# Softmax attention: the products for the maxima on two row groups of TensorE, from a second copy of the stacked queries and keys

## The reference

```
q = (x @ Wq).reshape(b, s, 2, 4, 16)      # s = 1024 tokens of an image
kk = (x @ Wk).reshape(b, s, 2, 16)
v = (x @ Wv).reshape(b, s, 2, 16)
scores = einsum('bqkgd,btkd->bkgqt', q, kk) / 4
attn = softmax(scores, axis=-1)
out = einsum('bkgqt,btkd->bqkgd', attn, v) @ Wo
```

## Time and profile before

| | |
|---|---|
| median of 3 runs | 4212.15 us (4211.81 to 4214.71) |
| profiled execution | 4220.6 us, its span 4218.9 us |
| TensorE matmuls | 3328.1 us busy, 79% |
| TensorE weight loads | 1655.9 us, 39% |
| VectorE | 2950.6 us, 70% |
| ScalarE | 2077.9 us, 49% |
| POOL | 1704.8 us, 40% |

### The profile page before, as it was taken

The page is one execution under the profiler, slowest core; times in us unless marked ns, Lnnn a source line. Parts: engine busy times, 40 slices in busy tenths (PEclk is TensorE's granted clock), DMA queues, the critical chain, the costliest instruction groups (busy, mean ns, idle before and its releaser), DMA issues. The chain is left out here.

```text
span 4218.9 us, 69037 instructions
## 1 busy us (share of the span) xinstructions
PE 3328.1 (79%) x20395; PEld 1655.9 (39%) x20397; DVE 2950.6 (70%) x6280; ACT 2077.9 (49%) x3690; POOL 1704.8 (40%) x2093
## 2 busy tenths in 40 slices
PE   2479999999999999999955999077877778638883
PEld 0212333333332333333224887045555555425552
DVE  7568887878788887888814666557766677546664
ACT  3326666666666666666644776011212212237772
POOL 2111232333232322333234554245666666437772
PEclk9769999999999999999987999589999999869995
DMA  2021111121101111121003332001111111033336
GB/s 94 18 33 25 27 39 37 39 41 40 37 25 26 39 38 38 40 40 39 12 14 112 104 104 95 12 24 37 39 39 38 36 38 38 25 104 102 103 99 255
DMA packets 122360, 226.28 MB, mean 54 GB/s; under 512 B 36048, under 2 KB 41416, under 8 KB 121880
## 3 DMA queue, kind: packets, MB, share of 16 engines
q1 hardware_dynamic: 82776, 142.33, 13.5%
q0 software_dynamic: 33664, 69.27, 5.2%
q10 hardware_dynamic: 5536, 9.99, 0.6%
HBM read 116.99 MB, written 104.50 MB: 52 GB/s over the span
## 5 line engine op out<-in xcount | busy, mean ns | idle before, releaser
L1217 ACT ACTIVATE b_probs<-b_ps_s 128x512 f32<-128x512 f32 x2048 | 1174.0, 596 | 678.0 <-PE b_ps_s L1261 639.4
L1019 DVE TENSOR_REDUCE b_maxes<-b_ps_m 128x1 f32<-128x1024 f32 x1024 | 1216.7, 1215 | 325.1 <-PE b_ps_m L1249 317.8
L1261 PE MATMUL b_ps_s<-b_qs,b_ks 99*128 99x512 bf16 x2048 | 789.8, 389 | 86.7 <-DMA b_qs<-b_m_parts 41.9
L1249 PE MATMUL b_ps_m<-b_ks,b_qs 96*128 96x512 bf16 x2048 | 639.8, 395 | 68.6 <-DVE b_maxes L1019 47.3
L1273 PE MATMUL b_ps_o<-b_probs,b_vs 128*32 128x512 f32 x4096 | 549.4, 609 | 23.3 <-ACT b_probs L1217 22.8
L1261 PEld LDWEIGHTS b_ps_s<-b_qs,b_ks 99*128 99x128 bf16 x2048 | 198.8, 98 | 884.5 <-ACT b_probs L1217 685.2
L938 POOL DMA_INDIRECT slots_in<-b_xn,b_slot x256 | 250.9, 980 | 416.4 <-ACT b_probs L1217 369.8
L1893 POOL DMA_INDIRECT pair_rows<-e_y_out,e_xin x284 | 284.5, 1002 | 131.9 <-issue 83.5
L2531 POOL DMA_INDIRECT cards_in<-d_cards,d_slot x256 | 251.7, 983 | 179.7 <-DVE d_slot L2809 93.0
L2463 POOL DMA_INDIRECT d_y<-slots_out,d_slot_now x256 | 246.3, 962 | 142.1 <-DVE d_inner L2694 65.2
L1249 PEld LDWEIGHTS b_ps_m<-b_ks,b_qs 96*128 96x128 bf16 x2048 | 191.8, 100 | 242.5 <-DVE b_maxes L1019 113.4
(11 more groups left out here) (493 smaller groups left out, 6423.2 us busy)
## 6 DMA issues: line engine op xcount, KB each, us to landing
b_qs<-b_q_parts SPq DMA_DIRECT2D x96, 256.0 KB, 8.4
e_xin<-cards_in SPq DMA_DIRECT2D x71, 260.0 KB, 2.8
c_xin<-slots_in SPq DMA_DIRECT2D x71, 256.0 KB, 2.6
slots_out<-c_y_out SPq DMA_DIRECT2D x71, 256.0 KB, 2.0
f_pairs<-pair_rows SPq DMA_DIRECT2D x32, 512.0 KB, 8.2
b_q_parts<-b_qparts SPq DMA_DIRECT2D x16, 768.0 KB, 3.4
a_x<-in_x_dram SPq DMA_DIRECT2D x8, 1024.0 KB, 10.0
out_dram<-f_turned ACTq DMA_DIRECT2D x16, 512.0 KB, 6.7
```

Source lines behind the costliest of these rows:

```text
L1019: nc.vector.tensor_reduce(maxes[:, kv, u:u + 1], ps_m[:, u % 2], AX.X, ALU.max).then_inc(m_free, 1)
L1217: nc.scalar.activation(probs[:, s % PROBS, j * HALF:(j + 1) * HALF], ps_s[:, j % 2], ACT.Exp).then_inc(exp_done, 1)
L1249: last = nc.tensor.matmul(ps_m[:, u % 2, half * HALF:(half + 1) * HALF], qs[0:STACK, buffer, h * PX + qt * P:h * PX + qt * P + P], ks[0:ST ...
L1261: nc.tensor.matmul(ps_s[:, j % 2], ks[0:rows, parity, kv * PX + tt * P:kv * PX + tt * P + P], qs[0:rows, parity, h * PX + half * HALF:h * ...
```

## The change

The products for the maxima use three of the six blocks (48 rows) instead of six. The first 512 keys are multiplied from rows 0 to 47 of qs and ks, the other 512 keys from rows 64 to 111 of two new tensors, qm and km, that hold a second copy of the same blocks. The two matmuls of a unit so use different rows of the array, and write different banks. SP fills the copy for image n+1 by twelve more DMAs an image, six for each kv: those of kv 0 go out behind the twelve stacking DMAs, those of kv 1 behind place_maxima(n, 1). Each six is preceded by a wait for the reductions that read the old contents. TensorE waits for the copy at the first unit of each kv. The maxima come from fewer parts, hence with a small error that the softmax divides out; the scores themselves are made as before.

```
--- before.py
+++ after.py
@@ -580,6 +580,7 @@
 STACK = 6 * DK
 SPLIT_Q = (0, 0, 1, 0, 1, 2)
 SPLIT_K = (0, 1, 0, 2, 1, 0)
+MAX_PARTS = 3
 STEPS = KV * 2 * TILES
 PROBS = 2
 MAXES = GROUP * TILES
@@ -628,6 +629,8 @@
         rest = sb("b_rest", [P, 2, HALF])
         qs = sb("b_qs", [P, 2, HEADS * PX], BF16)
         ks = sb("b_ks", [P, 2, KV * PX], BF16)
+        qm = sb("b_qm", [P, HEADS * PX], BF16)
+        km = sb("b_km", [P, KV * HALF], BF16)
         vs = sb("b_vs", [P, 2, TILES, KV, 2 * DK])
         maxes = sb("b_maxes", [P, KV, MAXES])
         m_parts = sb("b_mparts", [MAXES, 3, P], BF16)
@@ -683,6 +686,7 @@
         part2_done = sem("b_part2")
         part3_done = sem("b_part3")
         stacked = sem("b_stacked")
+        max_stacked = [sem(f"b_max_stacked{kv}") for kv in range(KV)]
         spilled = sem("b_spilled")
         m_spilled = sem("b_m_spilled")
         v_done = sem("b_v_done")
@@ -805,6 +809,20 @@
                 sp.wait_ge(m_spilled, 16 * n + 16)
                 sp.dma_start(qs[STACK:STACK + 3, buffer, cols], m_dram[buffer, :, cols]).then_inc(m_rows, 16)
 
+            def stack_for_maxima(n, kv, other):
+
+                positive(sp, m_free, (2 * n + kv + 1) * MAXES)
+                for g, part in enumerate(SPLIT_Q[:MAX_PARTS]):
+                    rows = slice(P // 2 + DK * g, P // 2 + DK * g + DK)
+                    sp.dma_start(
+                        qm[rows, kv * GROUP * PX:(kv + 1) * GROUP * PX].rearrange("d (h t) -> d h t", h=GROUP),
+                        q_dram[other, part].rearrange("(h d) t -> d h t", d=DK)[:, kv * GROUP:(kv + 1) * GROUP],
+                    ).then_inc(max_stacked[kv], 16)
+                for g, part in enumerate(SPLIT_K[:MAX_PARTS]):
+                    rows = slice(P // 2 + DK * g, P // 2 + DK * g + DK)
+                    sp.dma_start(km[rows, kv * HALF:(kv + 1) * HALF],
+                                 k_dram[other, part, kv * DK:(kv + 1) * DK, HALF:]).then_inc(max_stacked[kv], 16)
+
             def body(n, parity):
                 finish, prepare, steps = parts_of(n)
                 m = n + 1
@@ -826,8 +844,11 @@
                             ks[DK * g:DK * g + DK, other, :].rearrange("d (h t) -> d h t", h=KV),
                             k_dram[other, part].rearrange("(h d) t -> d h t", d=DK),
                         ).then_inc(stacked, 16)
+                    stack_for_maxima(n, 0, other)
                 if steps:
                     place_maxima(n, 1, parity)
+                if prepare:
+                    stack_for_maxima(n, 1, other)
                 if prepare:
                     place_maxima(m, 0, other)
 
@@ -1244,14 +1265,15 @@
 
             def max_unit(m, kv, u, buffer):
                 h, qt = kv * GROUP + u // TILES, u % TILES
+                if u == 0:
+                    pe.wait_ge(max_stacked[kv], 2 * MAX_PARTS * 16 * (m + 1))
                 positive(pe, m_free, (2 * m + kv) * MAXES + u - 1)
-                for half in range(2):
-                    last = nc.tensor.matmul(
-                        ps_m[:, u % 2, half * HALF:(half + 1) * HALF],
-                        qs[0:STACK, buffer, h * PX + qt * P:h * PX + qt * P + P],
-                        ks[0:STACK, buffer, kv * PX + half * HALF:kv * PX + half * HALF + HALF],
-                        start=True, stop=True)
-                last.then_inc(m_ready, 1)
+                rows, at = MAX_PARTS * DK, h * PX + qt * P
+                nc.tensor.matmul(ps_m[:, u % 2, 0:HALF], qs[0:rows, buffer, at:at + P],
+                                 ks[0:rows, buffer, kv * PX:kv * PX + HALF], start=True, stop=True)
+                nc.tensor.matmul(ps_m[:, u % 2, HALF:], qm[P // 2:P // 2 + rows, at:at + P],
+                                 km[P // 2:P // 2 + rows, kv * HALF:(kv + 1) * HALF], start=True, stop=True
+                                 ).then_inc(m_ready, 1)
 
             def scores(n, s, parity, j):
                 g, tt = s // TILES, s % TILES
```

## The result

The changed kernel takes 4236.38 us (median of 4 runs, 4235.27 to 4243.14) against 4212.15 before: ratio 1.0058, 95% interval [1.0039, 1.0077], so 24 us slower. The forecast was 4222, on the same side; it is 14 us short.

What follows compares the result with a forecast made beforehand. Taken as bound: attention, by TensorE's order and ScalarE's exponential, VectorE waiting for TensorE. Terms +6 - 2 + 3 + 3 = +10 us on the profiled 4220.6, 4230.6; less 8.45 to the median, 4222 us; range 4160 to 4285.

Steps and rivals of the forecast that it cites:

- Rivals 1, 2 and 4: Units: shape changes cheap (4122 or 4170, chance 0.20); half's weights load slowly (4274, 0.12); halves not abreast (4331, 0.05).
- "+6": Units for maxima in attention: saved pass spent on shape changes and exposed weights, 384 x 0.015 = +6 us.
- "-2": Units that waited for VectorE: the change of shape runs inside the wait, most taken back: -2 us.
- The copy, "+3": Wait for the second copy at step 12: 1.7 us an image, mostly hidden, 0.2 x 15 = +3 us.
- the first image's "+3": First image: TensorE already waits 18.1 us for its stack, without cover; the copy adds 3.0 us.
- "1.96 us of cover against 1.7": Step 12's wait of 1.7 us hidden by vanishing waits: 0.56 for VectorE, 1.40 for the row of maxima.
- Rival 3: Cover at step 16 fails: 1.7 x 15 = 26 us in place of the copy's +3, 4245; chance 0.08.

Runs made afterwards that it cites:

- experiment 1: Changed kernel with the old units (two matmuls over 96 stacked rows); the copy is made and waited for but not read: 4238.49 us, ratio 1.0063 to before.
- experiment 3: Changed kernel with its 48-row units, the copy made for the first image only (output not the reference's): 4221.95 us, ratio 1.0019 to before.
- experiment 11: Changed kernel with POOL splitting the row of maxima ahead of its normalising: 4223.32 us, ratio 1.0019 to before.
- experiment 2: Changed kernel with the old 96-row units, the copy made but neither waited for nor read: 4224.96 us, ratio 1.0027 to before.
- experiment 10: Kernel before, without the change, with POOL splitting the row of maxima ahead of its normalising: 4161.68 us, ratio 0.9882 to before.
- experiment 5: Changed kernel with eight 96-row products, their result overwritten, ahead of the wait for the copy at step 12: 4218.45 us, ratio 1.0022 to before.
- experiment 4: Changed kernel with both halves over the same 48 rows of the stack, no overlap and no copy: 4558.36 us, ratio 1.0807 to before.
- experiment 7: Changed kernel with the copy made for the first image only and products over 16 rows instead of 48: 4752.17 us, ratio 1.1304 to before.
- experiment 6: Changed kernel with maxima from one block of 16 rows, the copy a third as large: 4745.75 us, too scattered for a ratio.

## Why the prediction came out right

*The unit.* 0.65 us from S0 to S1 was forecast and 0.65 was found (1059.01, the start of S0 in the pair that begins at 1058.58, to 1059.66); Ma to S1 is 0.32; plain steps are 3.04 to 3.05; the halves start 0.00 to 0.01 apart. Rivals 1, 2 and 4 are out by these rows alone. Start to start, a change of shape costs 0.10 to 0.11 us over the 0.22 without one, weights included; 0.09 and 0.01 were forecast. The rule named in the prediction, that a change of tiling mode drains the engine (the Trainium skill, "TensorEngine Tiling (Array Packing)", Key Properties), agrees with the trace in so far as every change costs that much; that it is a drain no row here shows.

*The terms "+6" and "-2"* were a little high: steps 2 to 8, with a fill, came out 0.02 to 0.07 shorter, not 0.02 longer, and steps that wait for VectorE 0.2 shorter. Outside steps 11 to 16 the stage gives back 14.3 us after the change and 3.2 in experiment 1, so by the traces the units win some 11 us there. The win doesn't reach the time: experiment 3 takes 0 to 16 us more than before, and experiment 1 against the change says that the units cost and win nothing (1.0063 to 1.0058). A place where it can go is the clock: with 48 rows abreast the stage is at the lower level 44 us longer than before (experiment 3), and 54 us longer than in experiment 1 (the change), which is worth 22 and 27 us at most. That this is the place is argued. I can't settle a number closer than "no gain".

*The copy, "+3".* This is the term that was mis-sized; with the first image's "+3" it measured +24 to +27 (the change, experiment 1). The step of the prediction that failed is its last sentence on cover, "1.96 us of cover against 1.7", and it failed in three places, of which the cover is not one. The cover worked: b_m_parts fell by 28.4 us, and without it (experiment 11) the change costs 62.

First, the wait is 2.1 and not 1.7. The copy is not at fault: it lands 2.6 us behind the stack in the mean of 15 images, where 3.0 was forecast. What is gone is the 1.3 us of room between the stack's landing and Ma of step 12, for step 12 now waits for the stack itself in 10 images (3 before).

Second, the traffic also delays the stack, which the prediction left out: it placed the added transfers behind the old ones. The last stacking DMA lands 11.8 us behind its issue in the mean of 15 images after the change and in experiment 1, and 11.3 in experiment 2; in the kernels without a copy it is 10.7 (before), 11.0 (experiment 3) and 11.4 (experiment 10). Traffic that nobody waits for costs 11 us by itself (experiment 2). Not all of the longer wait for b_ks, 3.4 to 12.7, is the traffic's, though: experiment 10 makes no copy and has 9.1.

Third, and most in the changed kernel, the granted clock: the prediction said that an added idle might make it fall "in some images" and gave it "some us", outside its sum, with the argument that a wait of 1.40 had not done so. That was one image. The same trace has a shorter wait for the row of maxima behind which the clock does fall, right after 0.69 us of another wait (timeline, then the window):

```profile
630.37 1.06 PE L1273 MATMUL b_ps_o<-b_probs,b_vs 128*32 128x512 f32 x8 [0.69 <-ACT b_probs L1217]
632.82 0.39 PE L1261 MATMUL b_ps_s<-b_qs,b_ks 99*128 99x512 bf16 x1 [1.38 <-DMA b_qs<-b_m_parts]
...
633.20:636.60 3.40, 3.40 (x12) 1.57 (x10) 2.10 (x2) 2.13 (x4) 0.00 (x0) 0.51 0.00 0
```

The new wait likewise comes right behind the one for the stack, 0.99 and then 2.39 us in the image shown, and the clock falls in all 15 images. In the image shown TensorE then runs at 1.2 GHz from 1046.48, where the unit starts, to 1055.3. Experiment 5 gives that share: 15 of 24 us.

*The first image, "+3".* Its first unit came 2.9 us later (234.04 for 231.10), its first score only 0.8 (285.0 for 284.2): other work hid the rest.

*From the profiled execution to the median.* The sum was made for the profiled execution, 4230.6, and that came out at 4235.27, 4.7 us above. The other 10 of the 14 us are the step to the median: the prediction took off the 8.45 us by which the profiled execution before stood above its median, but single executions scatter by as much (20 runs of the kernel before, made beside experiments 1 to 4, lie between 4206.45 and 4229.76). After the change the profiled execution is 1.1 below the median.

*Rival 3*, that the cover fails and 26 us are lost, came near in size and is wrong in mechanism: had it been the cover, the wait for b_m_parts would have stayed at 41.9.

So the number came out right in part by luck. The unit and the cover are as forecast; the copy's term is not, and the range of 4160 to 4285 was wide enough, mostly for the rivals' sake, to hold a loss several times the one in the sum.

What stays open: how the 11 us of traffic that nobody reads divide (the wait for b_ks is +2.4, and 27 us more at the lower clock are worth 13 at most), and why the clock of the units alone differs so much from run to run. A smaller or later copy at 48 rows was not tried.

## What to carry to other kernels

Before a load is moved or added ahead of a tight reader, look not only for what hides the wait but for what TensorE does behind it: here most of the wait itself, 2.1 us an image, was given back at a later wait, and the slow clock that followed it was not. If work must wait, products whose result is thrown away, put ahead of the wait, gave back 15 of 24 us. The gain in this kernel lay elsewhere, on the engine that made the awaited row late: moving POOL's split ahead of 1.90 us of normalising, with no work saved, was worth 50 us.

## What the runs showed of the hardware

The time at the lower clock grows as the products use fewer rows. In the attention stage it was 55 us with units of 96 rows, 99 us with units of 48 rows abreast (experiment 3), 696 us with units of 48 rows one after the other (experiment 4) and 1519 us with 16 rows abreast (experiment 7). Between experiments 3 and 7 nothing but the rows differs. What grows most is how long a stretch lasts: 6.8 us at most before, up to 143 us in experiment 4 and up to 137 us in experiment 7, and TensorE is all but fully busy in them (54.00 of 54.00 us in experiment 4, 121.52 of 122.80 in experiment 6).

A wait isn't needed to set such a stretch off. In experiment 4 TensorE was busy for 3.40 of the 3.40 us before the clock fell at 1084.3, and its longest idle time in the 8 us before was 0.29. The page "TensorE: Matmul & The Clock Gate" of the Trainium skill, Part 1, ties the lower level to an engine that was idle. The trace agrees for the waits (0.50 from inside the 2.39 us wait, with TensorE busy for 3.06 of the 5 us before), but not here; the measurement decides. Why fewer rows lower the clock no run shows.
